# Early-fusion block on one core: bias rows stored ahead of the images, table in three transfers ahead of the norms, last pair's normed rows on VectorE

## The chip, the cores and the metric

The kernel runs on one core of a Trainium2 chip. The metric is the device time of one execution in microseconds (us); the time before is the median of three runs.

## What is computed

64 images of 3 x 224 x 224 and 64 texts of 32 rows become 64 sequences of 228 rows of 256 numbers; each goes through an attention block with a bias that depends on the distance of two rows, and all 14,592 rows then go through a mixture of eight experts that each pick their best rows. What matters for the change is the bias table:

```python
pos = jnp.arange(S, dtype=jnp.int32)
bucket = _rel_position_bucket(pos[None, :] - pos[:, None])
bias = rel_bias[bucket]                       # 32 buckets x 16 heads
attn = jnp.einsum('bqhd,bkhd->bhqk', q, k) + bias
attn = attn * scale[None, :, None, None]
attn = jnp.where(causal[None, None], attn, -1000000.0)
attn = jax.nn.softmax(attn, axis=-1)
```

and what follows the attention block, a norm over 256 numbers before the router: `h + ffn(_layernorm(h))`.

## The kernel before

**Two phases.** The first phase goes over 32 pairs of images, one pair in each trip: patches to rows (`tok1`, `tok2`), a first norm on DVE and POOL, q, k and v, attention over 16 groups of two heads, output projection, MLP, second norm, router. It is a software pipeline written out by hand: in trip i the PE does the front of pair i and the tail of pair i-1. `Part` and `ORDER` fix the order in which two PSUM banks (`G`) are filled and emptied. The second phase (from about 2,940 us) ranks the rows for each expert and runs the experts. Engines meet only by semaphores, and each engine's order is the order of its program.

**Setup, around the change.** SyncE (`@block.sync`) issues all large loads on its one queue: `w1t`, the first pair's images (`load_images(0)`, L687), their spread from `turned` to `img` (`spread_images(0)`, L695, in two halves, each after POOL has turned the images at L1699), the second pair's images, `w2t`, `b2t`, the text, `wqkv`. ScalarE's queue carries small vectors: `relb`, `sc_col`, `sc_bc`, `lnw`, `b1t`, then eight `fb1c` and two `fb2c` in pieces of 4 bytes (L978 to L987).

**The bias table.** DVE scales `relb` (L1213), which waits for all of ScalarE's small vectors, copies it into 31 runs of `zrow` (L1215; 16 heads x 455 distances, the first 228 of which are -3e38) and takes a running maximum `mrow` (L1217). SyncE stores `zrow` 114 times for each head (L727), each copy shifted by one more element, so that reading it back with the pitch gives one row of the table for each partition, and stores `mrow` (L729). Once both have landed, eight transfers load the table: for each half of the heads `bias_t[:, h, 0:S]` (114 x 8 x 228, L736), `bias_t[:, h, S:QW]` (114 x 8 x 114, L737) and the same two shapes of the maximum into the idle tiles `hT` and `qkT` (L738, L739), which are called `mtmp` here. Then four weights (L741), and only then the second pair's images are spread (L695).

DVE makes the table in `bias_table()`, which stands behind `qk_norm`: two subtractions (L1246), the scaling of `w1m` (L1250, waits for the four weights), and a memset behind ScalarE's `Exp` over the table (L1083). ScalarE reaches that `Exp` after `high_parts` (L1018). The heads' probabilities are multiplied by `bias_t` (L1395).

**First attention.** The PE's first transposes of it (`qkT`, L425) wait for DVE's `qk_norm` and for POOL's `high_parts_again` (L1691). In front of the latter POOL has `turn_images(1, 1)` (L1699), which waits until the first half of the second pair's images has been spread.

**Last pair.** Its second norm: DVE's statistics (L1261, L1264), POOL's reciprocal root (L1643) and four `tensor_scalar` of 114 x 256 on POOL (L1678) into `xn2` (the trace calls it `xn`), which the PE transposes (L359) for the router and SyncE stores (L714):

```python
step(rsqrt(rstd2[:, :], rstd2[:, :], NT), apart=True)
for t in range(NT):
    last = pool.tensor_scalar(xn2[:, t, :], hy[:, t, :], mv2[:, t, 0:1], rstd2[:, t:t + 1],
                              ALU.subtract, ALU.mult)
last.then_inc(xn2_done, 1)
```

Of the kernel before, what the change touches and what calls it, by code (L numbers as in the profile page):

```python
# [48 lines left out]
def early_fusion_kernel(nc, x, txt, tok_W1, tok_b1, tok_W2, tok_b2, ln1_w, Wq, Wk, Wv, rel_bias, scale, Wo,  # L49
# [10 lines left out]
    S = NP_ + TXT  # L60
    T = S // 2
    LASTP = NP_ - T
    N = B * S
    PAIRS = B // 2
    NT = 4
# [36 lines left out]
    with ctx:  # L102
# [3 lines left out]
        def sem(name):  # L106
            return ctx.enter_context(nc.semaphore(name))
# [79 lines left out]
        mtmp = [hT[0:T, :, :].rearrange("p m w -> p (m w)"), qkT[0:T, :, :, :].rearrange("p c s w -> p (c s w)").bitcast(F32)]  # L187
# [59 lines left out]
        pool_consts = sem("pool_consts")  # L247
        zrow_ready, rows_out, toeplitz_in = sem("zrow_ready"), sem("rows_out"), sem("toeplitz_in")
# [12 lines left out]
        ln2_stats, xn2_done = sem("ln2_stats"), sem("xn2_done")  # L261
# [411 lines left out]
        def _(sp):  # L673
# [43 lines left out]
            spread_images(0)  # L717
            load_images(1)
# [3 lines left out]
            for k, src in enumerate((Wq, Wk, Wv)):  # L722
# [3 lines left out]
            pitch = 2 * S - 1 + T  # L726
            sp.dma_start(bass.AP(zrow_d, 0, [[T * pitch, H], [pitch + 1, T], [1, 2 * S - 1]]),  # L727
                         zrow.unsqueeze(1).to_broadcast([H, T, 2 * S - 1])).then_inc(rows_out, 16)
            sp.dma_start(mrow_d[:, :], mrow).then_inc(rows_out, 16)  # L729
            sp.wait_ge(rows_out, 32)  # L730
            toep = lambda h, n: bass.AP(zrow_d, h * T * pitch + S - 1, [[pitch, T], [T * pitch, H // 2], [1, n]])
            mx = lambda h, o, n: bass.AP(mrow_d, h * S + o, [[0, T], [S, H // 2], [1, n]])
            for k in range(2):
                h = k * (H // 2)
                m = mtmp[k][:, 0:H // 2 * QW].rearrange("p (h q) -> p h q", q=QW)
                sp.dma_start(bias_t[:, h:h + H // 2, 0:S], toep(h, S)).then_inc(toeplitz_in, 16)  # L736
                sp.dma_start(bias_t[:, h:h + H // 2, S:QW], toep(h, T)).then_inc(toeplitz_in, 16)  # L737
                sp.dma_start(m[:, :, 0:S], mx(h, 0, S)).then_inc(toeplitz_in, 16)  # L738
                sp.dma_start(m[:, :, S:QW], mx(h, T, T)).then_inc(toeplitz_in, 16)  # L739
# [236 lines left out]
        def _(eng):  # L976
            with nc.allow_non_contiguous_dma(reason="small vectors of weights"):
                act.dma_start(relb[:, :], rel_bias.rearrange("k h -> h k")).then_inc(consts_in, 16)  # L978
                act.dma_start(sc_col[:, :], scale.rearrange("(h o) -> h o", o=1)).then_inc(consts_in, 16)
                act.dma_start(sc_bc[:, :], scale.partition_broadcast(T)).then_inc(consts_in, 16)  # L980
# [94 lines left out]
            act.wait_ge(consts_in, 16 * (6 + NE + KC))  # L1075
# [6 lines left out]
            act.wait_ge(table_diff, 1)  # L1082
# [112 lines left out]
        def _(eng):  # L1195
# [16 lines left out]
            dve.wait_ge(consts_in, 16 * (6 + NE + KC))  # L1212
# [20 lines left out]
            dve.memset(sc_q[0:1, 0:NT:2, :], 0.0)  # L1233
            dve.wait_ge(qkv_in, 16 * 3)
# [5 lines left out]
            def bias_table():  # L1240

                dve.wait_ge(toeplitz_in, 16 * 8)
                for k in range(2):
                    hs = slice(k * (H // 2), (k + 1) * (H // 2))
                    m = mtmp[k][:, 0:H // 2 * QW].rearrange("p (h q) -> p h q", q=QW)
                    last = dve.tensor_tensor(bias_t[:, hs, :], bias_t[:, hs, :], m, ALU.subtract)  # L1246
                last.then_inc(table_diff, 1)
# [119 lines left out]
            def mlp_stats(part):  # L1367
                part.wait_evacuated(dve, "w2", 1)
                stats(hy, mv2, ln2_stats)
# [44 lines left out]
            front_b(part, 0)  # L1414
            qk_norm(part, 0)
            bias_table()
# [22 lines left out]
            mlp_stats(part)  # L1439
            router_transposed(part)  # L1440
# [176 lines left out]
        def _(eng):  # L1617
# [55 lines left out]
            def second_norm(j):  # L1673
# [133 lines left out]
```

## Time and profile before

| | us |
|---|---|
| median of 3 runs | 4518.1 (4512.38 to 4521.21) |
| the profiled execution: its own time | 4522.34 |
| its span, first to last instruction | 4520.5 |
| mean granted TensorE clock | 0.949 of full speed |

The span is 1.8 us shorter than that execution's own time. In the profile PE is TensorE's matmuls, PEld its weight loads, DVE VectorE, ACT ScalarE, POOL GpSimd and SP SyncE; a name with a q is an engine's issuing side. All times below are counted from the start of the span.

### The profile page before, as it was taken

What the parts mean: (1) busy time and instruction counts of PE and PEld (TensorE: products, weight loads), DVE (VectorE), ACT (ScalarE), POOL (GpSimd) and SP (SyncE); (2) the same over time, 40 slices, a digit from 0 to 9 for tenths busy, and PEclk for the clock granted to TensorE, in tenths of its full rate; (3) what the DMA queues carried; (4) which work ended last, traced back from release to release, by engine and by line L of the source; (5) the groups of instructions that cost most, each with busy time, mean ns of one, the idle gap of its engine ahead of it and who ended that gap; (6) DMA issues with size and microseconds to landing.
All of it is one profiled execution on the core that took longest, in us unless ns stands there. A gap on an engine that the chain in (4) does not pass through costs nothing. (4 is left out here: it accounts for less than half of the span.)

```text
span 4520.5 us, 76799 instructions
## 1 busy us (share of the span) xinstructions
PE 3966.2 (88%) x26370; PEld 2347.5 (52%) x26370; DVE 2400.7 (53%) x4843; ACT 2034.7 (45%) x3373; POOL 1716.0 (38%) x1366
## 2 busy tenths in 40 slices
PE   2699999999899899999989989726999999999998
PEld 1455555555555555555555555414555555555554
DVE  3455555555555555555545555366555555555554
ACT  0344444444444444444434444223555655565654
POOL 1132223323222232332223232103766666666666
PEclk8799999999999999999999999857999999999999
DMA  7422212222221222222122120071333233333233
GB/s 114 76 38 37 47 32 41 42 36 38 35 47 34 40 43 33 38 35 47 34 40 47 30 43 15 17 190 42 56 51 64 46 63 64 47 63 63 46 46 46
DMA packets 302872, 222.26 MB, mean 49 GB/s; under 512 B 111524, under 2 KB 290182, under 8 KB 302710
## 3 DMA queue, kind: packets, MB, share of 16 engines
q1 hardware_dynamic: 183550, 157.86, 18.2%
q0 software_dynamic: 107264, 62.29, 8.9%
q10 hardware_dynamic: 11896, 0.05, 0.2%
q8 instruction: 89, 1.46, 0.1%
q14 instruction: 73, 0.60, 0.0%
HBM read 117.43 MB, written 63.57 MB: 40 GB/s over the span
## 5 line engine op out<-in xcount | busy, mean ns | idle before, releaser
L1395 DVE TENSOR_TENSOR pr<-pr,bias_t 114x684 f32<-114x684 f32 x512 | 439.0, 869 | 235.5 <-ACT pr L1027 231.0
L1574 DVE SCALAR_TENSOR_TENSOR hTs<-hTe,scales,hTs 128x456 f16<-128x456 f32 x514 | 322.6, 687 | 446.6 <-ACT hTs L1141 446.6
L505 PE MATMUL G<-w2m,hT 128*114 128x256 f32 x2048 | 521.9, 391 | 42.0 <-ACT hT L1066 22.2
L1744 POOL DMA_INDIRECT out_dram<-contrib,idx_cur x256 | 515.5, 2014 | 103.8 <-issue 77.4
L1027 ACT ACTIVATE pr<-SC 114x684 f32<-114x684 f32 x512 | 376.2, 742 | 368.5 <-PE SC L442 368.2
L900 PE MATMUL SC<-xgT,ws 128*128 128x456 f16 x2316 | 469.7, 358 | 0.0
L1737 POOL DMA_INDIRECT xg<-xn_rows,idx_cur x264 | 419.4, 1589 | 117.1 <-issue 60.0
L490 PE MATMUL G<-yT,w1m 128*128 128x456 f32 x1024 | 412.3, 551 | 10.5 <-ACT yT L973 10.5
L505 PEld LDWEIGHTS G<-w2m,hT 128*114 128x114 f32 x2048 | 338.0, 178 | 126.3 <-ACT hT L1066 43.4
L370 PE MATMUL G<-img,w1t 128*128 128x392 f32 x768 | 311.6, 523 | 51.0 <-DMA b2t<-in_L_tok_b_dram 50.1
L1675 POOL TENSOR_TENSOR rstd<-mv,ln_eps 114x4 f32<-114x4 f32 x32 | 7.0, 218 | 906.0 <-DVE mv L1264 906.0
L900 PEld LDWEIGHTS SC<-xgT,ws 128*128 128x128 f16 x2316 | 227.4, 98 | 221.2 <-issue 3.6
L1141 ACT ACTIVATE hTs<-hTe,scales 128x456 f16<-128x456 f32 x514 | 330.5, 669 | 0.0
L911 PE MATMUL Y<-hTs,ws 128*128 128x456 f16 x1536 | 306.3, 356 | 0.0
L911 PE MATMUL SC<-hTs,ws 128*128 128x456 f16 x1536 | 306.3, 356 | 0.0
L1134 ACT ACTIVATE hTe<-SC,fb1c,unscales 128x456 f32<-128x456 f32 x386 | 280.4, 727 | 55.1 <-PE SC L900 54.2
L490 PEld LDWEIGHTS G<-yT,w1m 128*128 128x128 f32 x1024 | 189.8, 190 | 180.1 <-issue 154.4
L1333 DVE COPY qkT<-G 128x912 f16<-128x912 f16 x128 | 81.0, 633 | 367.0 <-PE G L425 367.0
L1691 POOL CAST qkp<-qkraw 114x256 f16<-114x256 f32 x128 | 90.3, 742 | 446.0 <-DVE qkraw L1320 446.0
L1648 POOL TENSOR_TENSOR lt<-mv,ln_eps 114x4 f32<-114x4 f32 x32 | 6.4, 199 | 606.5 <-DVE mv L1264 606.5
L1699 POOL COPY turned<-raw 96x1568 f32<-96x1568 f32 x64 | 186.3, 2912 | 114.3 <-DMA img<-turned 66.5
L405 PE MATMUL G<-wqkv,xsT 128*114 128x512 f32 x512 | 226.7, 596 | 0.7 <-ACT xsT L973 0.7
(230 smaller groups left out, 6928.0 us busy)
## 6 DMA issues: line engine op xcount, KB each, us to landing
raw<-in_x_dram SPq DMA_DIRECT2D x192, 196.0 KB, 6.2
img<-turned SPq DMA_DIRECT2D x384, 98.0 KB, 2.8
we<-in_L_ffn_W_dram SPq DMA_DIRECT2D x34, 1024.0 KB, 7.6
out_dram<-hy SPq DMA_DIRECT2D x32, 456.0 KB
xn_rows<-xn SPq DMA_DIRECT2D x32, 456.0 KB
xg<-xn_rows,idx_cur POOLq DMA_INDIRECT x264, 3.8
out_dram<-contrib,idx_cur POOLq DMA_INDIRECT x256, 5.4
bias_by_distance<-pr SPq DMA_DIRECT2D x1, 3241.9 KB, 37.4
```

The costliest lines, as they stand in the source:

```text
L370: last = pe.matmul(part.g(*key)[:, 0:2 * NP_], w1t[:, k, m * 128:(m + 1) * 128], img[:, k, :, :].rearrange("p b n -> p (b n)"), start=k == ...
L490: last = pe.matmul(part.g("w1", m)[:, 0:W], w1m[:, c, m * 128:(m + 1) * 128], yT[:, c, :], start=c == 0, stop=c == KC - 1)
L505: last = pe.matmul(part.g("w2", b)[0:T, at:at + D], hT[:, m, t * T:(t + 1) * T], w2m[:, m, :], start=m == 0, stop=m == MC - 1)
L900: last = pe.matmul(RING[bank2(key)][:, 0:W], ws1[eb][:, wp, c, m * 128:(m + 1) * 128], xgT[:, xp, c, :], start=c == 0 and i == 0, stop=c = ...
L911: last = pe.matmul(RING[bank2(key)][:, 0:W], ws2[eb][:, wp, m, c * 128:(c + 1) * 128], hTs[:, hp, m, :], start=m == 0 and i == 0, stop=m = ...
L1027: act.activation(pr[g % 4][:, :, :], SC[g % 2][0:T, :, 0:QW], ACT.Exp).then_inc(exp_done, 1)
L1134: act.activation(hTe[:, m, :], RING[bank2(key)][:, 0:W], ACT.Gelu, bias=bias[:, at:at + 1] if isinstance(at, int) else bias[:, bass.ds(at, ...
L1141: act.activation(hTs[:, 0, m, :], hTe[:, m, :], ACT.Identity, scale=scale_at(scales, 2, e)).then_inc(h_high, 1)
L1395: dve.tensor_tensor(pr[g % 4][:, :, :], pr[g % 4][:, :, :], bias_t[:, 2 * pair:2 * pair + 2, :], ALU.mult).then_inc(probs_done, 1)
L1574: dve.scalar_tensor_tensor(hTs[:, 1, m, :], hTe[:, m, :], scale_at(scales, 2, e), hTs[:, 0, m, :], ALU.mult, ALU.subtract).then_inc(h_spli ...
L1737: pool.indirect_dma_start(out=xg[k4][:, t, :], out_offset=None, in_=xd[:, :], in_offset=bass.IndirectOffsetOnAxis(ap=idx_cur[k4][:, t:t + ...
L1744: pool.indirect_dma_start(out=out_rows, out_offset=bass.IndirectOffsetOnAxis(ap=idx_cur[k4][:, t:t + 1], axis=0), in_=contrib[k][:, t, :], ...
```

## The change

SyncE's order: the six loads that stood behind `load_images(1)` move ahead of `spread_images(0)`, and behind them the two stores of the bias rows; then come `spread_images(0)` and `load_images(1)`, then the table. The copies of `zrow` are 341 elements long in place of 455. The table comes by three transfers: `bias_t[:, :, 0:S]` in two halves and the maximum rows of all heads in one (114 x 3648) into `hT`. The part `S:QW` of the table is taken by DVE from `bias_t[:, :, 0:T]`. `relb`, `sc_col` and `sc_bc` have a semaphore of their own (`table_in`). `bias_table()` stands ahead of `qk_norm`, the scaling of `w1m` behind it. The last pair's four `tensor_scalar` are DVE's.

```diff
@@ sync @@
             load_images(0)
-            spread_images(0)
-            load_images(1)
             sp.dma_start(w2t[:, :, :], tok_W2.rearrange("(c p) n -> p c n", p=128)).then_inc(tok_in, 16)
...
             sp.wait_ge(zrow_ready, 1)
-            pitch = 2 * S - 1 + T
-            sp.dma_start(bass.AP(zrow_d, 0, [[T * pitch, H], [pitch + 1, T], [1, 2 * S - 1]]),
-                         zrow.unsqueeze(1).to_broadcast([H, T, 2 * S - 1])).then_inc(rows_out, 16)
+            pitch, reach = 2 * S - 1 + T, S - 1 + T
+            sp.dma_start(bass.AP(zrow_d, 0, [[T * pitch, H], [pitch + 1, T], [1, reach]]),
+                         zrow[:, S - T:2 * S - 1].unsqueeze(1).to_broadcast([H, T, reach])).then_inc(rows_out, 16)
             sp.dma_start(mrow_d[:, :], mrow).then_inc(rows_out, 16)
+            spread_images(0)
+            load_images(1)
             sp.wait_ge(rows_out, 32)
...
             for k in range(2):
                 h = k * (H // 2)
-                m = mtmp[k][:, 0:H // 2 * QW].rearrange("p (h q) -> p h q", q=QW)
-                sp.dma_start(bias_t[:, h:h + H // 2, 0:S], toep(h, S)).then_inc(toeplitz_in, 16)
-                sp.dma_start(bias_t[:, h:h + H // 2, S:QW], toep(h, T)).then_inc(toeplitz_in, 16)
-                sp.dma_start(m[:, :, 0:S], mx(h, 0, S)).then_inc(toeplitz_in, 16)
-                sp.dma_start(m[:, :, S:QW], mx(h, T, T)).then_inc(toeplitz_in, 16)
+                sp.dma_start(bias_t[:, h:h + H // 2, 0:S],
+                             bass.AP(zrow_d, h * T * pitch + T - 1, [[pitch, T], [T * pitch, H // 2], [1, S]])).then_inc(toeplitz_in, 16)
+            sp.dma_start(mtmp, mrow_d[:, :].rearrange("h s -> (h s)").partition_broadcast(T)).then_inc(toeplitz_in, 16)
@@ scalar @@
-            act.wait_ge(table_diff, 1)
+            act.wait_ge(table_diff, 2)
@@ vector @@
-            dve.wait_ge(consts_in, 16 * (6 + NE + KC))
+            dve.wait_ge(table_in, 16 * 3)
             step(dve.tensor_scalar(relb[:, :], relb[:, :], sc_col[:, 0:1], None, ALU.mult))
...
+            dve.wait_ge(consts_in, 16 * (3 + NE + KC))
             dve.wait_ge(qkv_in, 16 * 3)
...
             def bias_table():
-                dve.wait_ge(toeplitz_in, 16 * 8)
-                for k in range(2):
...
-                    last = dve.tensor_tensor(bias_t[:, hs, :], bias_t[:, hs, :], m, ALU.subtract)
-                last.then_inc(table_diff, 1)
+                dve.wait_ge(toeplitz_in, 16 * 3)
+                m = mtmp.rearrange("p (h q) -> p h q", q=S)
+                dve.tensor_tensor(bias_t[:, :, S:QW], bias_t[:, :, 0:T], m[:, :, T:S], ALU.subtract).then_inc(table_diff, 1)
+                dve.wait_ge(table_diff, 1)
+                dve.tensor_tensor(bias_t[:, :, 0:S], bias_t[:, :, 0:S], m, ALU.subtract).then_inc(table_diff, 1)
+
+            def scaled_weights():
                 dve.wait_ge(weights_in, 16 * 4)
...
             front_b(part, 0)
+            bias_table()
             qk_norm(part, 0)
-            bias_table()
+            scaled_weights()
             masked_probs(part, 0)
...
             mlp_stats(part)
+            dve.wait_ge(last_scales, 1)
+            dve.wait_ge(xn2_stored, 16 * (j + 1))
+            for t in range(NT):
+                last = dve.tensor_scalar(xn2[:, t, :], hy[:, t, :], mv2[:, t, 0:1], rstd2[:, t:t + 1],
+                                         ALU.subtract, ALU.mult)
+            last.then_inc(xn2_done, 1)
             router_transposed(part)
@@ gpsimd @@
-            def second_norm(j):
+            def second_norm(j, last=False):
                 pool.wait_ge(ln2_stats, j + 1)
                 step(pool.tensor_tensor(rstd2[:, :], mv2[:, :, 1], ln_eps[:, 0:NT], ALU.add))
+                if last:
+                    rsqrt(rstd2[:, :], rstd2[:, :], NT).then_inc(last_scales, 1)
+                    return
```

SyncE's queue in the setup, before, from the first images to the four weights (`pr` is the tile that holds `zrow` and `mrow`):

```order
L687 DMA raw<-in_x_dram 16x14x224 x6
L695 DMA img<-turned 128x1x196 x12
...
L723 DMA wqkv<-in_L_attn_Wv_dram 128x2x256
L727 DMA bias_by_distance<-pr 16x114x455
L729 DMA bias_row_maximum<-pr 16x228
L736 DMA bias_t<-bias_by_distance 114x8x228
L737 DMA bias_t<-bias_by_distance 114x8x114
L738 DMA hT<-bias_row_maximum 114x8x228
L739 DMA hT<-bias_row_maximum 114x8x114
...
L741 DMA wo<-in_L_attn_Wo_dram 128x2x256
```

and with the change (its line numbers are the new file's):

```order
L688 DMA raw<-in_x_dram 16x14x224 x6
L718 DMA w2t<-in_L_tok_W_dram 128x2x256
...
L722 DMA wqkv<-in_L_attn_Wv_dram 128x2x256
L726 DMA bias_by_distance<-pr 16x114x341
L728 DMA bias_row_maximum<-pr 16x228
L696 DMA img<-turned 128x1x196 x12
L688 DMA raw<-in_x_dram 16x14x224 x6
L734 DMA bias_t<-bias_by_distance 114x8x228 x2
L736 DMA hT<-bias_row_maximum 114x3648
L738 DMA wo<-in_L_attn_Wo_dram 128x2x256
```

The store of the rows now stands ahead of the first pair's spread images, and five table transfers are gone.

VectorE between the first norm and q and k, with the change:

```order
L1294 TENSOR_TENSOR xa<-h,mv,lt 114x256 x4
L1242 TENSOR_TENSOR bias_t<-bias_t,hT 114x16x114 [waits toeplitz_in]
L1244 TENSOR_TENSOR bias_t<-bias_t,hT 114x16x228 [waits table_diff]
L1301 TENSOR_TENSOR sqb<-qkraw 114x512 [waits evacuated0]
L1302 TENSOR_REDUCE ss<-sqb 114x32 [waits dve_step]
```

The two subtractions, and the wait for the table in front of them, now stand ahead of the squares of q and k; before they stood behind the last `qkp` of the norm.

## Rows read from the trace of the kernel before

**Rows 1.** The page, part 1: TensorE's busy time and share of the span.
```profile
PE 3966.2 (88%) x26370; PEld 2347.5 (52%) x26370; DVE 2400.7 (53%) x4843; ACT 2034.7 (45%) x3373; POOL 1716.0 (38%) x1366
```

**Rows 2.** Timeline of the first 190 us, SyncE's transfer issues: start, length, what.
```profile
23.60 13.10 SPq L695 DMA_DIRECT2D img<-turned  x12
...
36.74 3.09 SPq L687 DMA_DIRECT2D raw<-in_x_dram  x6
...
42.98 1.51 SPq L727 DMA_DIRECT2D bias_by_distance<-pr  x1
44.53 11.70 SPq L729 DMA_DIRECT2D bias_row_maximum<-pr  x1
...
82.38 0.27 SPq L736 DMA_DIRECT2D bias_t<-bias_by_distance  x1
...
123.41 16.07 SPq L695 DMA_DIRECT2D img<-turned  x12
```

**Rows 3.** Timeline, the other engines from 20 to 95 us; in brackets the idle time and its releaser.
```profile
20.78 2.79 POOL L1699 COPY turned<-raw 96x1568 f32<-96x1568 f32 x1 [17.58 <-DMA raw<-in_x_dram]
...
24.56 0.23 DVE L1213 TENSOR_SCALAR relb<-relb,sc_col 16x32 f32<-16x32 f32 x1 [18.76 <-DMA fb2c<-in_L_ffn_b_dram]
...
30.07 2.84 POOL L1699 COPY turned<-raw 96x1568 f32<-96x1568 f32 x1 [6.50 <-DMA img<-turned]
...
48.17 2.80 POOL L1699 COPY turned<-raw 96x1568 f32<-96x1568 f32 x1 [15.26 <-DMA raw<-in_x_dram]
...
50.09 11.04 PE L370 MATMUL G<-img,w1t 128*128 128x392 f32 x24 [50.09 <-DMA b2t<-in_L_tok_b_dram]
...
52.38 1.15 DVE L1236 TENSOR_SCALAR wqkv<-wqkv,lnw 128x768 f32<-128x768 f32 x2 [17.14 <-DMA wqkv<-in_L_attn_Wv_dram]
...
71.88 2.05 DVE L1288 TENSOR_SCALAR xs<-h,mv,lt 114x256 f32<-114x256 f32 x4 [3.64 <-POOL lt L1654]
73.85 1.38 DVE L1295 TENSOR_SCALAR xa<-h,mv,lt 114x256 f32<-114x256 f32 x4
...
80.75 0.69 DVE L1302 TENSOR_TENSOR sqb<-qkraw 114x512 f32<-114x512 f32 x1 [5.52 <-ACT qkraw L973]
...
94.56 1.28 ACT L1083 ACT_TABLE_LOAD   x1
```

**Rows 4.** The same timeline, from 124 to 139 us.
```profile
124.08 3.01 DVE L1246 TENSOR_TENSOR bias_t<-bias_t,hT 114x2736 f32<-114x2736 f32 x1 [26.96 <-DMA qkT<-bias_row_maximum]
...
130.04 4.76 ACT L1083 ACTIVATE bias_t<-bias_t 114x5472 f32<-114x5472 f32 x1 [34.19 <-DVE bias_t L1246]
...
132.83 2.87 POOL L1699 COPY turned<-raw 96x1568 f32<-96x1568 f32 x1 [60.01 <-DMA img<-turned]
...
137.19 0.92 PE L425 MATMUL G<-ident_h,qkp 114*128 114x114 f16 x8 [48.49 <-POOL qkp L1691]
138.14 0.92 ACT L991 COPY qkT<-G 128x912 f16<-128x912 f16 x1 [3.34 <-PE G L425]
```

**Rows 5.** Busy table of four stretches; the last three columns: TensorE clock, DMA share, GB/s.
```profile
84.00:121.00 37.00, 4.70 (x19) 3.04 (x17) 12.02 (x33) 5.62 (x9) 0.00 (x0) 0.63 0.42 131
52.50:80.00 27.50, 17.57 (x50) 9.88 (x50) 7.67 (x22) 3.53 (x5) 4.01 (x8) 0.81 0.89 101
121.00:128.00 7.00, 0.00 (x0) 0.00 (x0) 3.92 (x2) 0.00 (x0) 0.00 (x0) 0.50 1.07 329
140.00:160.00 20.00, 16.49 (x163) 10.17 (x162) 8.86 (x12) 9.08 (x13) 2.85 (x1) 0.54 0.57 73
```

**Rows 6.** DMA issues of the first 260 us: size, and time from issue to landing.
```profile
img<-turned SPq DMA_DIRECT2D x36, 98.0 KB, 2.8
bias_by_distance<-pr SPq DMA_DIRECT2D x1, 3241.9 KB, 37.4
```

**Rows 7.** Timeline at the end of the last pair, from 2924 to 2933 us.
```profile
2926.30 4.83 POOL L1678 TENSOR_SCALAR xn<-hy,mv,rstd 114x256 f32<-114x256 f32 x4
...
2931.18 1.02 PE L359 MATMUL G<-ident,xn 114*128 114x114 f32 x4 [9.21 <-POOL xn L1678]
```

More of the change, by code:

```diff
@@ L186, in early_fusion_kernel @@
         rstd2 = s1("rstd2", [T, NT])
-        mtmp = [hT[0:T, :, :].rearrange("p m w -> p (m w)"), qkT[0:T, :, :, :].rearrange("p c s w -> p (c s w)").bitcast(F32)]
+        mtmp = hT[0:T, :, :].rearrange("p m w -> p (m w)")
         p1.close()
@@ L247, in early_fusion_kernel @@
         pool_consts = sem("pool_consts")
+        table_in = sem("table_in")
         zrow_ready, rows_out, toeplitz_in = sem("zrow_ready"), sem("rows_out"), sem("toeplitz_in")
@@ L260, in early_fusion_kernel @@
         hy_done, y2_sums, r2_done = sem("hy_done"), sem("y2_sums"), sem("r2_done")
-        ln2_stats, xn2_done = sem("ln2_stats"), sem("xn2_done")
+        ln2_stats, xn2_done, last_scales = sem("ln2_stats"), sem("xn2_done"), sem("last_scales")
         h1_stored, xn2_stored = sem("h1_stored"), sem("xn2_stored")
@@ L977, in _ @@
             with nc.allow_non_contiguous_dma(reason="small vectors of weights"):
-                act.dma_start(relb[:, :], rel_bias.rearrange("k h -> h k")).then_inc(consts_in, 16)
-                act.dma_start(sc_col[:, :], scale.rearrange("(h o) -> h o", o=1)).then_inc(consts_in, 16)
-                act.dma_start(sc_bc[:, :], scale.partition_broadcast(T)).then_inc(consts_in, 16)
+                act.dma_start(relb[:, :], rel_bias.rearrange("k h -> h k")).then_inc(table_in, 16)
+                act.dma_start(sc_col[:, :], scale.rearrange("(h o) -> h o", o=1)).then_inc(table_in, 16)
+                act.dma_start(sc_bc[:, :], scale.partition_broadcast(T)).then_inc(table_in, 16)
                 act.dma_start(lnw[:, 0, :], ln1_w.rearrange("(c p) -> p c", p=128)).then_inc(consts_in, 16)
@@ L1073, in x2_transposed @@
                 act_evacuate(part, ("x2T", c), xsT[:, c, :])
-            act.wait_ge(consts_in, 16 * (6 + NE + KC))
+            act.wait_ge(consts_in, 16 * (3 + NE + KC))
             part = Part("first", 0)
@@ L1240, in bias_table @@
             def bias_table():
-                dve.wait_ge(toeplitz_in, 16 * 8)
-                for k in range(2):
-                    hs = slice(k * (H // 2), (k + 1) * (H // 2))
-                    m = mtmp[k][:, 0:H // 2 * QW].rearrange("p (h q) -> p h q", q=QW)
-                    last = dve.tensor_tensor(bias_t[:, hs, :], bias_t[:, hs, :], m, ALU.subtract)
-                last.then_inc(table_diff, 1)
+                dve.wait_ge(toeplitz_in, 16 * 3)
[4 more added lines that the diff above has]
+            def scaled_weights():
                 dve.wait_ge(weights_in, 16 * 4)
@@ L1731, in _ @@
             second_rms(PAIRS - 1)
-            second_norm(PAIRS - 1)
+            second_norm(PAIRS - 1, last=True)
             def gather(n, k4):
```

2 lines of the change are left out of this document (removed).

## The prediction

> **What bounds the kernel now.** I read the page first. TensorE is busy for 88% of the span [rows 1], and the change touches nothing that it does in the 31 trips or with the experts. So only the places where it stands still can give time, and the change reaches two of them: the start, and the end of the last pair. I read these in the timeline, SyncE's issues first, then what the other engines wait for.
>
> At the start, follow SyncE's queue [rows 2]. The first pair's images are spread from 23.60 on, the second pair's are loaded at 36.74, and only at 42.98 is the store of the bias rows issued, although VectorE had scaled the bias at 24.56 [rows 3]. The store lands 37.4 us later [rows 6], at 80.4. The eight table loads begin at 82.38 and the last lands at 124.08, where VectorE starts its subtractions [rows 2, 4]. That is 41.7 us for 4,873 KB (in KB of 1,024 bytes: half the heads x 114 partitions x 342 elements, four times). Behind them stand the four weights, then the spread of the second pair's images at 123.41 [rows 2]. POOL can therefore turn their other half only at 132.83 (to 135.70), then casts its q parts, and this releases the PE at 137.19 after 48.5 us of idle time [rows 4]. The table is no later than that: its Exp runs from 130.04 to 134.80, and ScalarE takes the first `qkT` at 138.14 [rows 4]. Both paths hang on the same queue. I take 138.14 as the mark that moves: behind it, the order of every engine is as before.
>
> **The start, step by step.** I work out when ScalarE takes its first `qkT` with the change.
>
> 1. *Rows store.* `relb` and the scales are the first three of ScalarE's 16 small transfers, and VectorE had waited for all 16 (24.56); so the rows are made long before the first images land, and the store is next on SyncE by then: six loads take it 3.1 us (39.83 to 42.98 [rows 2]). Ahead of the store stand the first images, landed at 20.78, and the six loads. Before, these six were all in 4.2 us after images that landed at 48.17 (52.38) [rows 3]. Now that is 25.0; ScalarE's tiny packets go on to 24.5, so I take 26. From that point the store took 28.0 us before (52.38 to 80.4). In that stretch nothing else ran: 101 GB/s at a DMA share of 0.89 [rows 5]. It is bytes that cost, so 341 for 455 elements makes 21.0 us, and the rows land at 47. If it is the number of pieces (1,824 as before), 28.0 us: 54.
> 2. *First images.* Their first half is spread behind the store and lands with it, some 2 us later, at 49.5. POOL turns the other half in 2.9 (52.4). Before, the first product could have had its images 6.0 us after such a turn: the issues end 3.8 us after it (32.91 to 36.70 [rows 2, 3]), the last of them lands 2.8 us after it was begun [rows 6], about 2.2 after that. So the PE starts at 58.4 and not at 50.09 [rows 3]: **8.3 us lost**, and with it the first norm, q, k and v.
> 3. *Second images.* Issued from 56.2, landed 11.4 us later as before (36.74 to 48.17 [rows 2, 3]): 67.6.
> 4. *Table.* The three transfers can move from about 65.6, two microseconds before that landing. They have 3,249 KB. The old eight moved 4,873 KB in 39.7 us and 2 us of landing, which is 122.7 KB per us; so 26.5 us and 2 to land: 94.1. The share of the DMA engines was only 0.42 then, at 131 GB/s, while a stretch with the weights had 329 GB/s at 1.07 [rows 5]. The new third transfer has long rows, like the weights, but 114 partitions, like the table. Bounds: 5.3 us for its 1,624 KB at the weights' rate, 13.2 at the table's. I take the table's, as it is the same partitions and the same source; the low end would give 8 us more.
> 5. *Norm behind the table.* VectorE ends `xa` at 75.23 + 8.3 = 83.5 and now waits for the table until 94.1: **10.6 us idle that it did not have**. Queued behind that wait is all of `qk_norm`, and for it wait ScalarE's `high_parts`, POOL's casts and the PE. The subtractions have the same 5,472 elements as before: 6.0 us, and 0.1 for the wait between them. `qk_norm` starts at 100.2.
> 6. *To the mark.* Before, from the first square at 80.75 to the end of `high_parts` at 94.56 were 13.8 us, of which 1.0 was waiting for q and k; those are ready now, so 12.8. Then the function table (1.3) and Exp (4.8) [rows 3, 4], 18.9 together. The mark comes at 119.1 and not at 138.14: **19.0 us won**.
>
> What this covers, and what if it did not: POOL's turn before the casts started 8.8 us after the table landed (132.83 to 124.08 [rows 4]). With the same weights in between it ends at 94.1 + 8.8 + 2.9 = 105.8, while the last scaled q comes 0.7 us ahead of the end of `high_parts` (113.0), at about 112; it has 6 us of slack. The scaling of `w1m` needs the weights, which land some 7 us behind the table (2,312 KB at 329 GB/s [rows 5]), and stands between `qk_norm` (115.6) and the memset that waits for Exp anyway: 1.5 us, hidden. The two waits on ScalarE's other vectors cost nothing; they land at 24.5 [rows 3] and are wanted after 30. The PE stands still from 97.0 (88.7 before, 8.3 later) to 115.6, some 18 us in place of 48.5. After the long stand it had a granted clock of 0.54 from 140 to 160 [rows 5], near its lower level of 1.2 GHz; I count the same ramp, and nothing gained.
>
> A rule that speaks against the third transfer: the Trainium skill, "DMA: Bandwidth & Descriptors", "Why a DMA increments its semaphore by 16 and not by 1", says that a transfer runs on the largest number of engines up to 16 that divides both slowest dimensions, which for 114 partitions is 6. The trace agrees: a share of 0.42 is close to 6/16. By the rule the transfer stays at the table's rate; without it the mark would come 8 us sooner.
>
> **The end of the last pair.** POOL's four operations last 4.83 us and the PE starts right behind them [rows 7]. On VectorE the same operation on 114 x 256 took 2.05 us for four, or 1.38 where POOL was not copying beside it [rows 3]. POOL is idle here, so 1.7: **3.1 us won** (2.8 to 3.4). VectorE had nothing to do at that time, and the waits that it takes on (the previous store, the scales) are over or were POOL's. Router, store and ranking follow in the same order, so all of it arrives.
>
> **Sum.** 19.0 + 3.1 = 22.1 us. The profiled execution has 4522.34 and would have 4500.2. It lies 4.2 above the median of the runs and above all three; from the median of 4518.1, the time is **4496.0**.
>
> **Rivals.**
>
> *Images not held back (12%).* If the spread passes the store in the queue, the first half is issued once SyncE is free at some 30 and the PE starts at 45. The second images land at about 55, the table at 81.5, the mark comes at 106.5: 31.6 won and 3.1, 4483. Against it: before, SyncE was held for 11.70 us behind the store's issue [rows 2]. The Trainium skill, same page, "Queues, rings and completion order", says that each DMA engine takes descriptors in ring order, though landing has no such order; by that rule the images wait.
>
> *Table cost by transfers in flight, not bytes (12%).* If the three take the eight's 41.7 us, the mark is 13.2 later: 8.9 won, 4509. For it: the third transfer is new in form, one long row for each partition. Against it: the DMA rate was steady over the eight.
>
> *Store not shortened (11%).* If pieces count and the loads are 4 us slower beside the tiny packets, everything is 11 later: 4507.
>
> *Slower: the wait ahead of the norm (5%).* Before, 14 us of norm work lay beside the table's loads; now it comes after. If the table lands later than 94.1 + 22.1 + 9 = 125, the kernel loses more than can be measured. That needs the store to land at 66 (37 us after the loads with a slower start) and the three transfers to take 41.7: table at 126, the mark at 151, 10 us lost, 4528. Against it: store and table have 25% and 33% fewer bytes.
>
> That a part does nothing is possible for the early rows themselves, if SyncE were not free for them; but nothing ahead of them waits.
>
> **The numbers.** The forecast has 60%, with its own range from 4490 (third transfer fast) to 4502 (store 6 us later). The whole range must leave out 2 in 10 at most: from 4483 to 4509, which takes in all but the slower rival and the edges. A measurement tells about 0.2%, 9 us, from no change. Faster by more: forecast, images not held, store not shortened and a third of the transfer rival, 0.87. Within: the rest of that one, late stores and clock, 0.09. Slower: 0.04.
>
> **What would show it.** The rows land near 47, the first product starts near 58 (later than before), VectorE waits some 10 us for the table behind `xa`, which lands near 94; the DMA share there stays near 0.42; ScalarE takes its first `qkT` near 119. Near the last pair's end four VectorE operations of 0.4 us stand in place of POOL's 4.83 us. I am wrong if the first product starts before 50, if the table lands after 105, or if the distance from the mark to the end changes by more than 5 us.

## The result, and the profile after

| | before | changed |
|---|---|---|
| median of 22 runs each, us | 4516.04 (4500.08 to 4530.46) | 4500.38 (4479.15 to 4512.86) |
| ratio, 95% interval | | 0.9968 [0.9955, 0.9981] |
| profiled execution's own time / span | 4522.34 / 4520.5 | 4512.86 / 4510.8 |
| mark: ScalarE's first `qkT` | 138.14 | 124.43 |
| last two stores of normed rows, interval | 63.14 | 59.84 |

The changed kernel is faster by 14.5 us (8.6 to 20.3); the difference of the medians is 15.7. The forecast was 22.1 us, and 4496.0 us with a range from 4483 to 4509. The time lies inside the range, but only about two thirds of the gain that was worked out is there. The two come out so differently because the kernel before had a median of 4518.1 us in the three runs that the forecast starts from and has 4516.04 in these 22: 2.1 us of the time's closeness are luck. The profiled execution happens to be the slowest of its 22, so whole spans are a poor comparison here; the mark and the last interval are sharper.

SyncE's queue in the timeline of the changed kernel (start, length, queue, line, what). It answers to [rows 2]:

```profile
13.06 1.69 SPq L726 DMA_DIRECT2D bias_by_distance<-pr  x1
14.79 12.87 SPq L728 DMA_DIRECT2D bias_row_maximum<-pr  x1
...
27.70 30.15 SPq L696 DMA_DIRECT2D img<-turned  x12
...
57.90 3.03 SPq L688 DMA_DIRECT2D raw<-in_x_dram  x6
...
60.97 9.25 SPq L734 DMA_DIRECT2D bias_t<-bias_by_distance  x2
...
70.27 6.02 SPq L736 DMA_DIRECT2D hT<-bias_row_maximum  x1
...
96.69 15.27 SPq L696 DMA_DIRECT2D img<-turned  x12
```

The rows' store is issued at 13.06 in place of 42.98. I read the row at 14.79 as the queue pushing back: a store of 16 short rows occupies SyncE for 12.87 us with the large one ahead of it, as it did for 11.70 before [rows 2]. The first pair's spread is therefore issued only from 27.70 on, 4.10 us later than before [rows 2], and the second pair's loads at 57.90 in place of 36.74.

The other engines, same view. In brackets stands the idle time and what ended it; it answers to [rows 3, 4]:

```profile
51.27 2.80 POOL L1708 COPY turned<-raw 96x1568 f32<-96x1568 f32 x1 [28.44 <-DMA img<-turned]
...
60.68 11.19 PE L371 MATMUL G<-img,w1t 128*128 128x392 f32 x24 [60.68 <-DMA img<-turned]
...
69.44 2.84 POOL L1708 COPY turned<-raw 96x1568 f32<-96x1568 f32 x1 [15.37 <-DMA raw<-in_x_dram]
...
84.61 1.37 DVE L1294 TENSOR_SCALAR xa<-h,mv,lt 114x256 f32<-114x256 f32 x4
...
96.61 2.06 DVE L1242 TENSOR_TENSOR bias_t<-bias_t,hT 114x1824 f32<-114x1824 f32 x1 [10.62 <-DMA hT<-bias_row_maximum]
...
98.70 3.96 DVE L1244 TENSOR_TENSOR bias_t<-bias_t,hT 114x3648 f32<-114x3648 f32 x1
...
102.58 0.68 DVE L1301 TENSOR_TENSOR sqb<-qkraw 114x512 f32<-114x512 f32 x1
...
105.38 2.80 POOL L1708 COPY turned<-raw 96x1568 f32<-96x1568 f32 x1 [21.80 <-DMA img<-turned]
105.46 3.27 DVE L1301 TENSOR_TENSOR sqb<-qkraw 114x512 f32<-114x512 f32 x1
...
114.90 2.90 DVE L1319 TENSOR_TENSOR qkraw<-qkraw,rn 114x512 f32<-114x512 f32 x4
...
119.76 4.76 ACT L1080 ACTIVATE bias_t<-bias_t 114x5472 f32<-114x5472 f32 x1
...
124.43 0.90 ACT L988 COPY qkT<-G 128x912 f16<-128x912 f16 x1
```

Two brackets carry the story. The PE's first product waits for `img`, and starts at 60.68 where it started at 50.09 [rows 3]: 10.6 us lost. VectorE waits 10.62 us for the maximum rows, and yet the table is subtracted at 96.61 in place of 124.08 [rows 4]: 27.5 us won. The mark nets 13.7 us. One row was not foreseen: the square at 105.46 lasts 3.27 us, its neighbour at 102.58 0.68, and POOL's copy of 2.80 us runs at the same moment.

The issues of the first 260 us (KB each, median us from issue to landing), for [rows 6]:

```profile
bias_by_distance<-pr SPq DMA_DIRECT2D x1, 2429.6 KB, 32.3
```

The store lands at 45.4. The busy table of three stretches (start:end, length, busy us and instructions of PE, PEld, DVE, ACT and POOL; then granted TensorE clock, DMA share, GB/s), for [rows 5]:

```profile
28.00:45.00 17.00, 0.00 (x0) 0.00 (x0) 0.00 (x0) 0.00 (x0) 0.00 (x0) 1.00 0.90 99
72.00:77.00 5.00, 3.68 (x16) 2.56 (x16) 1.44 (x4) 0.50 (x1) 0.28 (x1) 1.00 0.41 137
...
164.00:174.00 10.00, 8.38 (x37) 6.08 (x35) 4.80 (x17) 0.98 (x2) 3.93 (x8) 0.83 0.20 36
```

The store moves 99 GB/s at a share of 0.90, the table 137 at 0.41: nearly the two rates of before (101 at 0.89, 131 at 0.42 [rows 5]). The table's stretch ends before the four weights are issued, at 76.33.

The end of the last pair, from the timeline, for [rows 7]:

```profile
2923.08 1.38 DVE L1443 TENSOR_SCALAR xn<-hy,mv,rstd 114x256 f32<-114x256 f32 x4 [1.40 <-POOL rstd L1649]
...
2924.52 1.02 PE L360 MATMUL G<-ident,xn 114*128 114x114 f32 x4 [5.71 <-DVE xn L1443]
```

Four operations in 1.38 us stand in place of POOL's 4.83, and the PE starts right behind them.

### The profile page after: what moved, and what is told of

Its sections match the earlier page's. It is cut to its first block and busy times, and to the rows that moved or that the text cites. A ratio compares the mean times of both kernels' runs of the same rounds, so it can differ in the third digit from the quotient of the medians.

```text
span 4510.8 us, 76796 instructions
## 1 busy us (share of the span) xinstructions
PE 3977.8 (88%) x26370; PEld 2348.5 (52%) x26370; DVE 2406.6 (53%) x4847; ACT 2036.6 (45%) x3373; POOL 1701.1 (38%) x1362
## 5 line engine op out<-in xcount | busy, mean ns | idle before, releaser
L1753 POOL DMA_INDIRECT out_dram<-contrib,idx_cur x256 | 550.8, 2152 | 112.1 <-issue 80.9
L491 PE MATMUL G<-yT,w1m 128*128 128x456 f32 x1024 | 412.2, 551 | 10.6 <-ACT yT L970 10.6
L1746 POOL DMA_INDIRECT xg<-xn_rows,idx_cur x264 | 368.1, 1394 | 117.3 <-issue 60.3
L1301 DVE TENSOR_TENSOR sqb<-qkraw 114x512 f32<-114x512 f32 x128 | 91.2, 712 | 254.0 <-ACT qkraw L970 253.9
## 6 DMA issues: line engine op xcount, KB each, us to landing
bias_by_distance<-pr SPq DMA_DIRECT2D x1, 2429.6 KB, 32.3
```

Of the source, the lines that this page charges most:

```text
L491: last = pe.matmul(part.g("w1", m)[:, 0:W], w1m[:, c, m * 128:(m + 1) * 128], yT[:, c, :], start=c == 0, stop=c == KC - 1)
L1746: pool.indirect_dma_start(out=xg[k4][:, t, :], out_offset=None, in_=xd[:, :], in_offset=bass.IndirectOffsetOnAxis(ap=idx_cur[k4][:, t:t + ...
L1753: pool.indirect_dma_start(out=out_rows, out_offset=bass.IndirectOffsetOnAxis(ap=idx_cur[k4][:, t:t + 1], axis=0), in_=contrib[k][:, t, :], ...
```

## The experiments

Each is an edit of the changed kernel unless said otherwise. e1 to e4 ran on one chip, e5 to e8 on a second, e9 to e11 on a third, each with runs of the kernel before beside it; all but e6 and e10 are single runs. The same program's mark differs by some 2 us from one chip and execution to another: 124.43 and 122.81 for the changed kernel (e11), 138.14 and 135.92 for the old start (e5). The first product differs by 3: it comes at 60.68, 59.34, 58.16, 61.12 and 59.25 in the changed kernel, e11, e1, e3 and e4, which have the same code up to there. So a change behind the first product is better read from the distance between that product and the mark, 63.75 us in the changed kernel and 63.47 in e11. Smaller differences of marks are not read.

### e1: the table behind the norm again

```diff
-            bias_table()
             qk_norm(part, 0)
+            bias_table()
             scaled_weights()
```

> The changed kernel with bias_table() behind qk_norm again, all else as changed. Theory (the wait for the table in front of the norm costs time, since q and k are ready 11 us before the table's subtractions end): qk_norm starts near 91.6 us and ends near 108, the subtractions end near 114, Exp near 119, and ScalarE takes its first qkT near 119 in place of 124.4. Rival (the early table is what lets ScalarE's Exp run early, so that it pays): the mark comes at 125 or later.

Mark 117.85. Timeline:

```profile
88.33 0.69 DVE L1301 TENSOR_TENSOR sqb<-qkraw 114x512 f32<-114x512 f32 x1 [5.36 <-ACT qkraw L970]
...
102.84 6.49 POOL L1708 COPY turned<-raw 96x1568 f32<-96x1568 f32 x1 [22.29 <-DMA img<-turned]
...
106.70 6.45 DVE L1244 TENSOR_TENSOR bias_t<-bias_t,hT 114x3648 f32<-114x3648 f32 x1
...
117.85 0.90 ACT L988 COPY qkT<-G 128x912 f16<-128x912 f16 x1
```

The norm starts at 88.33, as soon as q and k are there. The mark is 5.0 to 6.6 us earlier than with the change, but 1.2 to 2.5 of this are an earlier first product (58.16), which the edit does not touch. From there to the mark are 59.7 us in place of 63.5 to 63.7: the edit is worth some 4 us. So the part "table ahead of the norm" costs time by itself; the rest of the change pays for it. The gain could be larger, but now the long subtraction and POOL's copy hold each other: 6.45 in place of 3.96 and 6.49 in place of 2.80.

### e2: SyncE's old order, with the shorter rows and the three transfers

```diff
             load_images(0)
+            spread_images(0)
+            load_images(1)
             sp.dma_start(w2t[:, :, :], tok_W2.rearrange("(c p) n -> p c n", p=128)).then_inc(tok_in, 16)
...
             sp.dma_start(mrow_d[:, :], mrow).then_inc(rows_out, 16)
-            spread_images(0)
-            load_images(1)
```

> The changed kernel with SyncE's old order: first pair spread and second pair loaded, then the six loads, then the two stores; three table transfers and the early subtractions stay. Theory (storing the rows first brings the table forward but delays the first product): first product at 50 in place of 60.7, store of the rows lands near 73, the table near 104 in place of 96.6, the mark near 130 to 132. Rival (the order gives nothing, the fewer bytes do it all): the mark stays within 2 us of 124.4.

Timeline:

```profile
49.28 10.96 PE L371 MATMUL G<-img,w1t 128*128 128x392 f32 x24 [49.28 <-DMA b2t<-in_L_tok_b_dram]
...
103.29 2.06 DVE L1242 TENSOR_TENSOR bias_t<-bias_t,hT 114x1824 f32<-114x1824 f32 x1 [28.96 <-DMA hT<-bias_row_maximum]
...
130.31 0.90 ACT L988 COPY qkT<-G 128x912 f16<-128x912 f16 x1
```

The PE starts at 49.28, the table is subtracted at 103.29 after 28.96 us of waiting, and the mark is 130.31. The early store is worth 5.9 us of the mark's 13.7, fewer bytes and the rest 7.8; against e11's mark and e5's the two are 7.5 and 5.6.

### e3: the table's transfers cut into 112 and 2 partitions

```diff
-                sp.dma_start(bias_t[:, h:h + H // 2, 0:S],
-                             bass.AP(zrow_d, h * T * pitch + T - 1, [[pitch, T], [T * pitch, H // 2], [1, S]]))...
+                for lo, n in ((0, 112), (112, T - 112)):
+                    sp.dma_start(bias_t[lo:lo + n, h:h + H // 2, 0:S],
+                                 bass.AP(zrow_d, h * T * pitch + T - 1 + lo * pitch, [[pitch, n], ...
```

and the maximum rows in the same way.

> The changed kernel with each of the three table transfers cut into one of 112 partitions and one of 2. Theory (114 partitions put a transfer on 6 of the 16 DMA engines, which is why the share was 0.42): the share rises to 0.9 or more while the table is loaded, the table lands near 81 in place of 96.6, VectorE no longer waits for it behind xa (ends 86.0), and the mark comes near 112 to 115. Rival (the share is low because of what is read, short pieces and one row for all): the table lands within 3 us of 96.6.

Mark 112.90. The busy table and the timeline:

```profile
70.00:83.00 13.00, 5.53 (x22) 3.32 (x20) 3.70 (x13) 0.59 (x1) 6.32 (x9) 0.88 1.07 283
```

```profile
84.56 1.37 DVE L1298 TENSOR_SCALAR xa<-h,mv,lt 114x256 f32<-114x256 f32 x4
85.85 2.05 DVE L1246 TENSOR_TENSOR bias_t<-bias_t,hT 114x1824 f32<-114x1824 f32 x1
...
112.90 0.90 ACT L992 COPY qkT<-G 128x912 f16<-128x912 f16 x1
```

The subtraction has no bracket: the table is there before VectorE asks, 10.8 us earlier than with the change. The DMA share in this stretch is 1.07, at 283 GB/s, where it was 0.41 and 137 in the changed kernel; but here the four weights, issued from 70.00 on, move beside the table, so these two rows do not compare the same bytes. The single packets in the two traces do, with weights beside them in both: the 114 long rows of the maximum (1,624 KB) move from 81.76 to 96.09 in the changed kernel and from 74.59 to 82.15 with the cut, 116 GB/s and 220. This is the sharpest result of the study, from nothing but a partition count. The Trainium skill, "DMA: Bandwidth & Descriptors", "Why a DMA increments its semaphore by 16 and not by 1", gives this: the slowest dimensions of 114 divide by 6 engines at most, those of 112 by 16. The trace agrees: 0.41 is close to 6/16, and with the cut the load is no longer held to it.

### e4: POOL's casts ahead of its copy

```diff
-            turn_images(1, 1)
             high_parts_again(0)
+            turn_images(1, 1)
```

> The changed kernel with POOL's high_parts_again(0) ahead of turn_images(1, 1). Theory (the square of q and k that took 3.27 us in place of 0.69 was held by POOL's copy of 2.80 us beside it): that square takes 0.69 again, the norm ends 2.6 us sooner and the mark comes at 121.9 in place of 124.4; the next pair's images are still there in time. Rival (something else held it, the spread's transfers for one): a square of over 3 us stays, and so does the mark.

Mark 120.26. Timeline:

```profile
104.65 0.69 DVE L1301 TENSOR_TENSOR sqb<-qkraw 114x512 f32<-114x512 f32 x1
...
113.72 3.00 POOL L1708 COPY turned<-raw 96x1568 f32<-96x1568 f32 x1
113.96 2.84 DVE L1327 COPY qkp<-qkp 114x256 f16<-114x256 f16 x1
...
120.26 0.92 ACT L988 COPY qkT<-G 128x912 f16<-128x912 f16 x1 [0.56 <-PE G L426]
```

All four squares take 0.69 us now, this being the last, and the long row has moved to whatever VectorE does beside the copy: `qkp` at 113.96. The stall goes where the copy goes. From the first subtraction (94.35) to the mark are 25.9 us in place of 27.8 (27.5 in e11). Up to the end of `Exp` the whole 2.6 us of the square are gained; 0.6 of it is lost again at the mark, where ScalarE now waits for the PE and the PE for the `qkp` that was held.

### e5: the kernel before with only the last pair changed

```diff
             mlp_stats(part)
+            dve.wait_ge(last_scales, 1)
+            dve.wait_ge(xn2_stored, 16 * (j + 1))
+            for t in range(NT):
+                last = dve.tensor_scalar(xn2[:, t, :], hy[:, t, :], mv2[:, t, 0:1], rstd2[:, t:t + 1], ...
...
-            second_norm(PAIRS - 1)
+            second_norm(PAIRS - 1, last=True)
```

On POOL's side `second_norm` ends behind the reciprocal root, as in the change.

> The kernel before with the last pair's normed rows on VectorE and nothing else changed. Theory (the whole gain of that part is POOL's 4.83 us against VectorE's 1.4): from the end of the reciprocal root to the PE's transpose 1.5 us in place of 5.0, and the distance from the last but one to the last store of normed rows is 3.3 to 3.5 us shorter than with POOL (63.14) at the same clock; the start of the kernel stays, first qkT at 138. Rival (the early start shifts the end too): the distance does not change.

```profile
2925.52 1.38 DVE L1443 TENSOR_SCALAR xn<-hy,mv,rstd 114x256 f32<-114x256 f32 x4 [1.40 <-POOL rstd L1649]
...
2926.96 1.02 PE L359 MATMUL G<-ident,xn 114*128 114x114 f32 x4 [5.71 <-DVE xn L1443]
```

The last interval is 59.60 in place of 63.14: 3.5 us, and the two parts of the change add up without touching each other.

### e8: rows of 455 elements again

```diff
-            pitch, reach = 2 * S - 1 + T, S - 1 + T
+            pitch, reach = 2 * S - 1 + T, 2 * S - 1
...
-                         zrow[:, S - T:2 * S - 1].unsqueeze(1).to_broadcast([H, T, reach])
+                         zrow[:, 0:2 * S - 1].unsqueeze(1).to_broadcast([H, T, reach])
...
-                             bass.AP(zrow_d, h * T * pitch + T - 1, ...
+                             bass.AP(zrow_d, h * T * pitch + S - 1, ...
```

> The changed kernel with copies of the bias row 455 elements long, as before. Theory (bytes cost, 99 GB/s): the store lands 7 to 8 us later (37 to 40 us after its issue in place of 32.3), and with it the first images, the first product (68 in place of 60.7), the table and the mark (132 in place of 124.4). Rival (pieces cost, and they stay 1,824): nothing moves by more than 2 us.

```profile
bias_by_distance<-pr SPq DMA_DIRECT2D x1, 3241.9 KB, 40.0
```

```profile
68.15 10.70 PE L371 MATMUL G<-img,w1t 128*128 128x392 f32 x24 [68.15 <-DMA img<-turned]
...
103.34 2.06 DVE L1242 TENSOR_TENSOR bias_t<-bias_t,hT 114x1824 f32<-114x1824 f32 x1 [10.41 <-DMA hT<-bias_row_maximum]
```

The same 1,824 pieces with a third more bytes take 40.0 us in place of 32.3, and 7.5 us of it reach the PE; the mark is 130.96, 6.5 later (8.2 against e11). The store costs by bytes: 812 KB in 7.7 us is 108 GB/s, close to the 99 of the stretch above.

### e9 and e11: ten transfers of tiny pieces away from the start

`fb1c` and `fb2c` are wanted by the experts only. e9 issues them on SyncE's queue near the last pair; e11 is the changed kernel again, on the same chip.

```diff
             load_text(PAIRS - 1)
...
+                for e in range(NE):
+                    sp.dma_start(fb1c[:, e, :], fb1[e].rearrange("(m p) -> p m", p=128)).then_inc(late_in, 16)
...
-                for e in range(NE):
-                    act.dma_start(fb1c[:, e, :], fb1[e].rearrange("(m p) -> p m", p=128)).then_inc(consts_in, 16)
```

> The changed kernel with the experts' ten small vectors (fb1c, fb2c, 10,240 pieces of 4 bytes) taken off ScalarE's queue at the start and issued by SyncE near the last pair. Theory (these pieces share the DMA engines with the first loads and the rows' store, which landed 32.3 us after its issue although 2,430 KB at 99 GB/s are 25.1): the first images land by 15 in place of 20, the store some 27 us after its issue, the first product comes near 54 to 56 in place of 60.7, the mark near 118 to 120 in place of 124.4; VectorE's two products that took 3.5 us are early and short. Rival (small pieces do not slow the large transfers): first images at 20 and first product within 1.5 us.

> The changed kernel once more, unchanged, beside the other two on the same chip. It gives how far the mark differs from chip to chip: between 122.5 and 125 if the kernels so far (start of the first product 58.2 to 61.1 with the same code up to there) differed by the chip alone.

The issue of the rows' store in e11's timeline:

```profile
13.71 1.47 SPq L726 DMA_DIRECT2D bias_by_distance<-pr  x1
```

And e9's timeline, which begins with the same issue:

```profile
11.04 1.48 SPq L726 DMA_DIRECT2D bias_by_distance<-pr  x1
...
17.26 2.80 POOL L1710 COPY turned<-raw 96x1568 f32<-96x1568 f32 x1 [14.06 <-DMA raw<-in_x_dram]
...
56.12 10.47 PE L371 MATMUL G<-img,w1t 128*128 128x392 f32 x24 [56.12 <-DMA img<-turned]
...
119.26 0.90 ACT L989 COPY qkT<-G 128x912 f16<-128x912 f16 x1
```

The first images are there at 17.26, not by 15 as expected, and the store takes 29.8 us, not 27: two misses. But the PE starts 3.2 us earlier than e11's 59.34 and the mark comes 3.5 earlier than 122.81. The 3.2 us come from the store's earlier issue (2.7 us) and its shorter time to landing (29.8 for 30.5); from the store's landing to the product are 15.1 us in e11 and 15.3 in e9. So forty KB in 4-byte pieces on another engine's queue cost some 3 us here, in the first loads and their issue. With the scatter of 3 us in the first product the size is uncertain, but 56.12 lies below all five values above.

### e6, e7 and e10: what the experiments point to

e6 puts the gains together: the six loads first, the first pair's spread ahead of the rows' store, the second pair's loads behind it; the table cut at 112; the table behind the norm; POOL's norm work and casts ahead of its turns. e7 is e6 without the cut; e10 is e6 with e9's edit. The order of SyncE's and POOL's work, shortened:

```diff
 sync:
             load_images(0)
             ...six loads...
+            spread_images(0)
             ...the two stores of rows...
-            spread_images(0)
             load_images(1)
 gpsimd:
-            turn_images(1, 0)
             first_norm(0)
             keep_h0(0)
-            turn_images(1, 1)
             high_parts_again(0)
+            turn_images(1, 0)
+            turn_images(1, 1)
```

> The changed kernel with: the six loads first, then the first pair's images spread, then the store of the rows, then the second pair's images and the table; table transfers cut at 112 partitions; subtractions behind the norm; POOL's norm scales and casts ahead of its turns of the second pair. Theory: first product near 38, norm of q and k from 69 to 86, table landed near 82, mark at 96 to 100 (with one stall of VectorE behind POOL's copy), 24 to 28 us before the changed kernel's 124.4; the whole 35 to 45 us below the kernel before. Rival (the later trips take up what the start gains): the mark comes early, but the first store of normed rows at 236.7 moves by less than half of that.

> The combined kernel, but with the three table transfers of 114 partitions. Theory (six DMA engines for 114 partitions): share near 0.4 while the table loads, table landed 13 to 16 us later than with the cut, near 96, and the mark near 107 to 110. Rival (with the images out of the way the transfers are fast anyway): within 3 us of the combined kernel.

> The combined kernel with the ten small vectors moved in the same way. Theory: everything at the start comes 4 to 6 us sooner than in the combined kernel, first product near 33, mark near 94 in place of 99.8. Rival (the store of the rows and the table are now what ends last, not the images): the first product comes sooner, the mark by less than 2 us.

e6's timeline:

```profile
38.67 9.95 PE L371 MATMUL G<-img,w1t 128*128 128x392 f32 x24 [38.67 <-DMA img<-turned]
...
68.39 0.69 DVE L1305 TENSOR_TENSOR sqb<-qkraw 114x512 f32<-114x512 f32 x1 [5.67 <-ACT qkraw L974]
...
89.10 2.04 DVE L1246 TENSOR_TENSOR bias_t<-bias_t,hT 114x1824 f32<-114x1824 f32 x1
...
99.84 0.90 ACT L992 COPY qkT<-G 128x912 f16<-128x912 f16 x1
```

and the one row in which e7 differs:

```profile
97.32 2.06 DVE L1242 TENSOR_TENSOR bias_t<-bias_t,hT 114x1824 f32<-114x1824 f32 x1 [7.91 <-DMA hT<-bias_row_maximum]
```

| | first product | table subtracted | mark | median us | ratio to before |
|---|---|---|---|---|---|
| changed | 60.68 | 96.61 | 124.43 | 4500.38 | 0.9968 [0.9955, 0.9981] |
| e6 | 38.67 | 89.10 | 99.84 | 4482.71 (7 runs) | 0.9924 [0.9896, 0.9952] |
| e7 | 38.37 | 97.32 | 108.08 | 4488.54 (one run) | |
| e10 | 36.13 | 86.14 | 96.88 | 4464.75 (5 runs) | 0.9890 [0.9873, 0.9906] |

With the small pieces gone as well, e10 is 1.1% faster than the kernel before, and its interval does not meet that of the change: it beats both kernels. Its mark misses its expected 94 by 3 us and its first product the expected 33 by as much: against e6 it gains 3.0 us at the mark, not 4 to 6, and the intervals of the two overlap, so what the small pieces alone are worth in the whole time is not shown. e7 shows the cut at 112 to be worth 8.2 us in this version. In e6 the store of the first pair's normed rows comes 38.7 us earlier than before, the mark 38.3: here the later trips keep all of it.

## Why the prediction was right, and where it was not

**Step 1, rows store.** Right. Forecast 47, measured 45.4; e8 shows that bytes cost and not pieces.

**Step 2, first images and first product.** Mechanism right, size off by 2.3: 60.68 for 58.4. The term that was mis-sized is the spread's, "lands with it, some 2 us later": 2.5 us were counted from the store's landing to the images, and 5.9 measured (45.4 to 51.27). Before, with nothing ahead of it, the same half had been issued at 23.60 and was there at 30.07 [rows 2, 3], so it needs some 6 us of its own, and none of it was hidden behind the store. The same distance is 5.7 in e11, 5.8 in e8 and 5.9 in e9. It makes 3.4 us more; the store came 1.6 sooner than 47, and from POOL's turn to the product were 6.6 us for 6.0.

The tiny pieces are not the reason, since e9 has the same 5.9 without them. They were taken to be done by 24.5 as before, but beside the store their issue stretched. In the timeline of the kernel before it is 16.88 us long, in that of the changed one 35.26:

```profile
4.19 16.88 ACTq L985 DMA_DIRECT2D fb1c<-in_L_ffn_b_dram  x8
```

```profile
4.17 35.26 ACTq L982 DMA_DIRECT2D fb1c<-in_L_ffn_b_dram  x8
```

So "they land at 24.5" was wrong: VectorE waits for them until 51.55 before it scales `wqkv`, which cost nothing, as `wqkv` is wanted only behind `xa`. What the pieces do cost, some 3 us (e9), they cost ahead of the store.

**Step 3, second images.** 69.44 for 67.6: only step 2's delay, less 0.5.

**Step 4, table.** Right: 27.2 us from those images to the subtraction, where 26.5 were worked out; it lands at 96.6 for 94.1, again step 2's delay. Share and rate were 0.41 and 137 GB/s, but only until the weights came: they moved beside the table and not behind it, and from 80 to 85 the share was 1.09. The low bound, the weights' rate for long rows (329 GB/s makes 5.1 us of 1,624 KB, not 5.3), fell: e3 shows that the partition count decides, and not the row's length.

**Step 5, VectorE behind the table.** Right: 10.62 us of waiting for 10.6.

**Step 6, from the norm to the mark.** This is the step that failed, by an overlap that it left out: "13.8 us, of which 1.0 was waiting for q and k; those are ready now, so 12.8". From the first square (102.58) to the end of `high_parts` (118.45) were 15.9 us. Of the 3.1 missing, 2.6 are the one square that ran beside POOL's copy. Before, that copy ran at 132.83, after the subtractions and beside nothing of VectorE's on the path [rows 4]; the text gave POOL's own end 6 us of slack and never asked what the copy does to VectorE. e4 takes the copy away and the square is back at 0.69; e1 shows the same hold on another pair of operations. Another 0.4 are the four `qkraw` behind it, 2.90 us (114.90), where they took 2.50 before:

```profile
91.39 2.50 DVE L1320 TENSOR_TENSOR qkraw<-qkraw,rn 114x512 f32<-114x512 f32 x4
```

With the change POOL's casts of q run beside them, from 115.66 on; in e1, where those casts come after, they take 2.5 again. The trace of before had a sign that a copy of POOL's slows VectorE: `xs` took 2.05 us and `xa`, the same operation, 1.38 [rows 3]. The prediction used it for the tail alone.

**The sum at the start.** 2.4 us by the norm's later start (102.58 for 100.2) and 3.0 from there to the mark (21.9 for 18.9) make it 124.43 for 119.1: 13.7 us won for 19.0.

**The tail.** 3.3 us for 3.1 (3.5 alone in e5): right.

**Behind the mark.** The two profiles lie 13.7 us apart at the mark but 11.75 at the first store of normed rows (248.40 to 236.65). This is not the change's doing: in e11, the same program, that store comes at 232.96, 110.15 us behind the mark, as in the kernel before (110.26), where the changed kernel's profile has 112.22. What differs is the granted clock. It was 0.83 from 164 to 174 and 1.00 in the same work before (178 to 188) and in e11 (162.4 to 172.4): the PE had been at the full level of 2.4 GHz for some 20 us and fell back for a few. The same dip stands in e1, e8 and e10, with distances of 111.81, 112.21 and 112.21; e2 and e9 have none, and 110.19 and 110.16. Why some executions have it stays open, and no run sets the clock. With 13.7 and 3.3 the measured gain should be 17.0, with 11.75 it is 15.1, and with e11's first store 18.7; the interval from 8.6 to 20.3 holds all three and excludes the forecast's 22.1.

**The signs of being wrong.** The first product did not start before 50, and the table did not land after 105. The third, a distance from the mark to the end that changes by more than 5 us, was not met either, but it says little: 4382.4 us before and 4386.4 in the changed kernel's profile, 4.0 longer where 3.1 shorter was expected, and 4370.6 in e11, with the same program, by which it would have been met. What makes this distance scatter stands in the last section.

**The rivals.** *Images not held back* fell: issued at 27.70, landed at 51.2. *Transfers in flight, not bytes* fell: the table was there at 96.6 and not at 107.3. *Store not shortened* fell with e8. *Slower, the wait ahead of the norm* has its mechanism (e1: some 4 us for that part) but its price stayed far under what the rest gained.

## What to carry to other kernels

Before a large transfer, look at its partition count: cutting 114 into 112 and 2 nearly doubled the rate of a load here (116 to 220 GB/s) and brought the mark 8 to 12 us forward, for three more instructions. When an operation is moved to where VectorE works, count what a GpSimd copy beside it does to VectorE, not only when that copy ends. Where whole times scatter by more than the effect, choose a mark close behind the change and compare that.

## What was not expected

**VectorE and GpSimd hold each other, whole instruction by whole instruction.** With the change, the copy runs from 105.38 to 108.18, and the square that is issued at 105.46 ends at 108.73, one length of 0.69 behind it, less a little. In e4 the 16-bit copy at 113.96 (0.21 us where nothing disturbs it) ends at 116.80, with POOL's copy at 116.72. In e1 VectorE's first subtraction was running from 104.61 to 106.66; POOL's copy, issued at 102.84, ends 2.7 us after that, at 109.33, and the long subtraction ends 3.82 us after that, at 113.15. So each waited out the other's instruction and then ran at nearly its own length (2.80 and 3.96). But the copy waited for more than one: from 102.84 to 106.66 it was passed by several operations of VectorE's of 0.2 to 0.4 us each, and by the first subtraction. Which of the two gets the next turn, no run shows. The Trainium skill, "SBUF — State Buffer", "SBUF: two separate sides", describes such a lock: of a GpSimd operation that reads SBUF and a VectorE operation with two SBUF inputs, or of a GpSimd operation and a VectorE one in a mode that uses two ports, whichever starts first gets the shared ports for its whole instruction and the other stands still. The traces agree for the squares and subtractions, which have two inputs; whether the 16-bit copy was in such a mode no trace shows. By that rule step 6 could have been priced before the run.

**The trips have two lengths.** The first 30 of the 31 intervals between stores of normed rows sum to 2,619.6 us before and to 2,628.0 with the change, though nothing in those trips was changed. Most are 86.6 to 88.2 us long, some about 85.4. e4 has twelve short ones, the changed kernel's profile none, the one before two. Two stretches at the boundary of a trip in e4, the first in a long trip, the second in a short one (busy table, clock third from the end):

```profile
319.90:328.70 8.80, 7.58 (x56) 3.21 (x59) 1.82 (x4) 3.12 (x6) 2.72 (x1) 0.61 0.17 53
1194.87:1203.67 8.80, 7.22 (x82) 4.11 (x83) 3.41 (x6) 5.50 (x8) 2.77 (x1) 1.00 0.17 53
```

In the long trip the granted clock falls towards its lower level of 1.2 GHz for this stretch; in the short one it stays at the full one. Over the 30 intervals the profiles differ by up to 31.6 us (2,596.36 in e3, 2,628.0 with the change), more than the whole change gives. It explains why e3 and e4, with single times of 4460.44 and 4469.47, look better than their marks can pay for, and why only marks, and distances from them, are read above. Which executions get the short trips stays open: e3 and e4 ran on one chip, but so did e1 and e2, which had two each. The profiled execution of the change lost 8.4 us of the pair's difference over these trips, some 4 of them for want of two short ones.
